# First attention: 1792 of 1857 softmax weights cross partitions by DMA, in runs of 448 keys

## The reference, cut to what matters

```python
k = (concat([ctx, x_normed]) @ Wk)      # 1857 keys, 4 groups of 128
v = (concat([ctx, x_normed]) @ Wv)
q = (x_normed @ Wq)                     # 32 heads of 128, 8 heads per group
scores = einsum('bqhgd,bkhd->bhgqk', q, k) / sqrt(128)
attn   = softmax(scores)                # float32
out    = einsum('bhgqk,bkhd->bqhgd', attn, v) @ Wo
```

## Time and profile before

| | |
|---|---|
| median of 3 runs | 3180.78 us (3176.02 to 3182.16) |
| the profiled execution | 3190.52 us, span 3188.8 us |
| its mean granted TensorE clock | 0.977 of full speed |
| busy shares of the span | PE 95%, PEld 85%, DVE 66%, ACT 54%, POOL 28% |
| DMA | 497 MB, 156 GB/s over the span |

### The profile page before, as it was taken

How to read it: one execution, slowest core, us unless ns; L and a number is a source line. 1 busy time by engine, 2 the same in 40 slices (tenths; PEclk the granted TensorE clock), 3 DMA queues, 4 the chain that set the end, 5 groups by cost and what they waited for, 6 DMA issues and landing times. The chain is left out here.

```text
span 3188.8 us, 54146 instructions
## 1 busy us (share of the span) xinstructions
PE 3040.3 (95%) x18566; PEld 2702.9 (85%) x18566; DVE 2104.0 (66%) x3215; ACT 1733.4 (54%) x3277; POOL 908.0 (28%) x742
## 2 busy tenths in 40 slices
PE   8999998999999999999999999979989799998897
PEld 7888887899999999899998999968768788886786
DVE  4433343788888888788887888854454567766675
ACT  4433344676666666666666666642243344443472
POOL 0000121344444444444444444432200124440101
PEclk9999999999999999999999999999989799999998
DMA  7665696766777776677766777557540111111683
GB/s 253 216 214 200 207 289 200 152 159 161 165 160 158 163 157 164 150 165 158 160 160 155 160 158 163 127 148 238 190 160 32 57 29 41 41 41 30 236 289 129
DMA packets 375894, 497.03 MB, mean 156 GB/s; under 512 B 34316, under 2 KB 283452, under 8 KB 375640
## 3 DMA queue, kind: packets, MB, share of 16 engines
q1 hardware_dynamic: 373080, 485.40, 56.8%
q0 software_dynamic: 2560, 8.39, 0.8%
HBM read 225.57 MB, written 133.87 MB: 113 GB/s over the span
## 5 line engine op out<-in xcount | busy, mean ns | idle before, releaser
L725 POOL TENSOR_TENSOR a_t_lo<-a_turned,a_t_hi 128x512 fp32r<-128x512 f32 x512 | 649.7, 1291 | 937.9 <-ACT a_t_hi L854 937.9
L845 ACT ACTIVATE a_probs<-a_ps_s,a_neg_max 128x1024 f32<-128x1024 f32 (+1 forms) x512 | 529.2, 1034 | 474.7 <-DVE a_neg_max L897 468.8
L890 DVE TENSOR_REDUCE a_half_max<-a_ps_s 128x1 f32<-128x1024 f32 (+1 forms) x512 | 571.1, 1115 | 190.9 <-PE a_ps_s L742 186.7
L740 PE MATMUL a_ps_s<-a_k_buf,a_q_buf 128*128 128x512 f32 (+1 forms) x1024 | 420.1, 410 | 17.9 <-ACT a_probs L845 11.9
L741 PE MATMUL a_ps_s<-a_k_buf,a_q_buf 128*128 128x512 f32 (+1 forms) x1024 | 385.7, 377 | 0.0
L742 PE MATMUL a_ps_s<-a_k_buf,a_q_buf 128*128 128x512 f32 (+1 forms) x1024 | 384.8, 376 | 0.0
L926 DVE TENSOR_TENSOR a_x_lo<-a_ps_x,a_x_hi 128x512 fp32r<-128x512 f32 (+1 forms) x512 | 314.3, 614 | 106.6 <-ACT a_x_hi L863 106.6
L916 DVE STREAM_TRANSPOSE a_turned<-xn 128x512 f32<-128x512 f32 x512 | 357.4, 698 | 0.0
L472 DVE TENSOR_TENSOR p_out<-p_ps_j,p_out 128x512 fp32r<-128x512 f32 (+3 forms) x196 | 153.3, 782 | 302.4 <-ACT p_out L400 302.4
L400 ACT ACTIVATE p_out<-p_ps_j 128x512 fp32r<-128x512 f32 (+3 forms) x196 | 141.9, 724 | 311.4 <-PE p_ps_j L293 311.4
L740 PE MATMUL a_ps_o<-a_t_hi,a_v_buf 128*128 128x256 f32 x1024 | 298.8, 292 | 6.1 <-issue 3.6
(11 more groups left out here) (394 smaller groups left out, 7102.0 us busy)
## 6 DMA issues: line engine op xcount, KB each, us to landing
xn<-a_probs SPq DMA_DIRECT2D x1024, 128.0 KB, 3.4
a_q_all<-p_out SPq DMA_DIRECT2D x64, 512.0 KB
a_q_buf<-a_q_all SPq DMA_DIRECT2D x128, 256.0 KB, 3.2
a_k_buf<-a_k_all SPq DMA_DIRECT2D x64, 464.5 KB, 4.0
a_v_all<-p_out SPq DMA_DIRECT2D x56, 512.0 KB
a_k_all<-p_out SPq DMA_DIRECT2D x48, 384.0 KB
a_v_buf<-a_v_all SPq DMA_DIRECT2D x64, 256.0 KB
a_o_all<-a_o_part SPq DMA_DIRECT2D x128, 128.0 KB, 3.1
```

Source lines behind the costliest of these rows:

```text
L725: pool.tensor_tensor(t_lo[:, slot, :, :], turned[:, slot, :, :], t_hi[:, slot, :, :].bitcast(F32), ALU.subtract).then_inc(t_done, 1)
L740: pe.matmul(o, w_hi, m_hi, start=first, stop=False)
L845: act.activation(probs[j][u.a][:, lo:hi], s_flat[:, lo:hi], ACT.Exp, bias=neg_max[:, j:j + 1], scale=SCALE, accum_out=half_sum[:, bass.ds( ...
L890: dve.reduce_max(half_max[:, half:half + 1], s_flat[:, lo:hi], AX.X).then_inc(max_done, 1)
```

## The change

The run grows from 256 to 448 keys, so 1792 keys go by the first way (seven steps per unit) and the last 65 by the second (one step, two transposes). The four DMAs per tile stay four, with rows of 1792 instead of 1024 bytes. `traded` gets a buffer of its own for odd units. The value loads become four of 32 partitions (14 blocks each) and one of 65. The rings of t_hi and t_lo keep four slots, that of x_hi and x_lo goes from four to two. A tile's transfers now wait for both halves of its exponentials. The output copy moves from VectorE to ScalarE, and every engine's order is rewritten. The core of the diff:

```diff
-    RUN = 256
+    RUN = 448
-    RING, PRING, XBANKS = 4, 4, 2
+    RING, PRING, XBANKS = 4, 2, 2
-    VALUE_PIECES = [(0, 1), (2, 3), (4,), (5, 6)]
+    VALUE_PIECES = [(0, 1), (2,), (3,), (4,)]
 load_values(sp, b, g, a, c):
-                elif c < RUNS + 2:
-                    lo, hi = [(0, VPLAIN), (VPLAIN, PLAIN - 1)][c - RUNS]
...
 trade(u, j):
-                    sp.wait_ge(probs_done, 4 * u.n + 2 * j + 1)
+                    sp.wait_ge(probs_done, 4 * u.n + 2 * j + 2)
 POOL step(b, r):
-                    w, l = Unit(b, r - 2), Unit(b, r - 3)
-                    low(l, 1)
-                    low(l, 2)
-                    low(l, 3)
-                    low(w, 0)
+                    for p in range(TPAIRS):
+                        low(Unit(b, r), p)
 TensorE step(b, r): v = r-1, w = r-2, l = r-3, z = r-4
+                    turn_plain(l, 0)
                     weigh_turned(z, 2)
-                    weigh_plain(z, 2)
-                    turn_plain(l, 1)
-                    weigh_plain(z, 3)
+                    weigh_turned(z, 3)
+                    weigh_turned(z, 4)
+                    weigh_turned(z, 5)
                     scores(v, 0, 0)
-                    turn_plain(l, 2)
                     scores(v, 0, 1)
-                    weigh_turned(z, 3, last=True)
-                    turn_plain(l, 3)
+                    weigh_turned(z, 6, last=True)
                     weigh_turned(l, 0, first=True)
                     weigh_plain(l, 0)
                     weigh_turned(l, 1)
                     scores(v, 1, 0)
-                    turn_plain(w, 0)
                     scores(v, 1, 1)
-                    weigh_plain(l, 1)
 ScalarE step(b, r): u = r, v = r-1, w = r-2, z = r-3
                     exponentials(v, 1, 0)
-                    plain_high(w, 1)
+                    plain_high(w, 0)
                     exponentials(v, 1, 1)
                     turned_high(w, 0)
                     turned_high(w, 1)
-                    plain_high(w, 2)
+                    turned_high(w, 2)
                     exponentials(u, 0, 0)
-                    plain_high(w, 3)
                     exponentials(u, 0, 1)
-                    turned_high(w, 2)
+                    take_output(z)
                     turned_high(w, 3)
-                    plain_high(v, 0)
+                    turned_high(w, 4)
+                    turned_high(w, 5)
+                    turned_high(w, 6)
 VectorE step(b, r): v = r-1, l = r-3
-                    plain_low(l, 1)
+                    turn_traded(l, 0)
                     turn_traded(l, 1)
+                    plain_low(l, 0)
+                    turn_traded(l, 2)
                     maximum(v, 0, 0)
                     maximum(v, 0, 1)
                     negate_maximum(v, 0)
-                    turn_traded(l, 2)
-                    take_output(z)
-                    plain_low(l, 2)
                     turn_traded(l, 3)
+                    turn_traded(l, 4)
+                    turn_traded(l, 5)
+                    turn_traded(l, 6)
                     maximum(v, 1, 0)
-                    plain_low(l, 3)
                     maximum(v, 1, 1)
                     negate_maximum(v, 1)
-                    plain_low(w, 0)
-                    turn_traded(w, 0)
```

More of the change, by code:

```diff
@@ L538, in grouped_attention_block @@
     pair_tiles = lambda e: range(2 * e, min(2 * e + 2, PLAIN))
-    RING, PRING, XBANKS = 4, 4, 2
+    RING, PRING, XBANKS = 4, 2, 2
     KPIECES = 4
-    VPLAIN = (PLAIN - 1) // 2
-    VALUE_PIECES = [(0, 1), (2, 3), (4,), (5, 6)]
+    VALUE_PIECES = [(0, 1), (2,), (3,), (4,)]
     PIECE = 2 * WIDTH // KPIECES
     VPIECES = sum(len(p) for p in VALUE_PIECES)
-    assert QT == 2 and len(CHUNKS) == 4 and HPG == 8 and TURNED <= 2 * BANK and TBLOCKS % 2 == 0 and WIDTH % 2 == 0
+    assert QT == 2 and len(CHUNKS) == 4 and HPG == 8 and TPAIRS == 7 and PPAIRS == 1 and TBLOCKS % 2 == 0 and WIDTH % 2 == 0
     assert PLAIN % 2 == 1 and TPAIRS * HEADS % RING == 0 and PPAIRS * HEADS % XBANKS == 0 and PPAIRS * HEADS % PRING == 0
@@ L582, in load_values @@
                                  keys_of[RUN * c:RUN * (c + 1), g, :].rearrange("(k i) d -> i k d", i=SQ)).then_inc(v_loaded[a], 16)
-                elif c < RUNS + 2:
-                    lo, hi = [(0, VPLAIN), (VPLAIN, PLAIN - 1)][c - RUNS]
-                    sp.dma_start(v_buf[a][:, TBLOCKS + lo:TBLOCKS + hi, :].bitcast(F32),
-                                 keys_of[TURNED + P * lo:TURNED + P * hi, g, :].rearrange("(m i) d -> i m d", i=P)
-                                 ).then_inc(v_loaded[a], 16)
                 else:
@@ L606, in grouped_attention_block @@
             probs = [[sb(f"probs{j}{a}", [P, KEYS]) for a in range(2)] for j in range(QT)]
-            traded = xn[:, :, :].rearrange("p t d -> p (t d)")[:, 0:2 * QT * TURNED].rearrange("p (a j g r) -> p a j g r", a=2, j=QT, g=RUNS)
+            by_run = lambda rows: rows.rearrange("p (j g r) -> p j g r", j=QT, g=RUNS)
+            traded = [by_run(xn[:, :, :].rearrange("p t d -> p (t d)")[:, 0:QT * TURNED]),
+                      by_run(sb("traded", [P, QT * TURNED])[:, :])]
             turned = sb("turned", [P, RING, 2, TOK])
@@ L663, in trade @@
                     for c in range(RUNS):
-                        sp.dma_start(traded[SQ * c:SQ * (c + 1), u.a, j, :, :], probs[j][u.a][:, RUN * c:RUN * (c + 1)]
+                        sp.dma_start(traded[u.a][SQ * c:SQ * (c + 1), j, :, :], probs[j][u.a][:, RUN * c:RUN * (c + 1)]
                                      ).then_inc(trade_done[j][u.a], 16)
@@ L728, in step @@
                 def step(b, r):
-                    w, l = Unit(b, r - 2), Unit(b, r - 3)
-                    low(l, 1)
-                    low(l, 2)
-                    low(l, 3)
-                    low(w, 0)
-                run(pool, step, 4)
+                    for p in range(TPAIRS):
+                        low(Unit(b, r), p)
+                run(pool, step, 0)
             @block.tensor
@@ L812, in step @@
                 def step(b, r):
-                    v, w, l, z = Unit(b, r - 1), Unit(b, r - 2), Unit(b, r - 3), Unit(b, r - 4)
+                    v, l, z = Unit(b, r - 1), Unit(b, r - 3), Unit(b, r - 4)
+                    turn_plain(l, 0)
                     weigh_turned(z, 2)
-                    weigh_plain(z, 2)
-                    turn_plain(l, 1)
-                    weigh_plain(z, 3)
+                    weigh_turned(z, 3)
+                    weigh_turned(z, 4)
+                    weigh_turned(z, 5)
                     scores(v, 0, 0)
-                    turn_plain(l, 2)
                     scores(v, 0, 1)
-                    weigh_turned(z, 3, last=True)
-                    turn_plain(l, 3)
+                    weigh_turned(z, 6, last=True)
                     weigh_turned(l, 0, first=True)
@@ L864, in plain_high, with take_output @@
                                    ).then_inc(x_hi_done, 1)
+                def take_output(u):
+                    if not u.live:
+                        return
+                    act.wait_ge(tv_ps, TPAIRS * (u.n + 1))
+                    act.wait_ge(xv_ps, PPAIRS * (u.n + 1))
+                    wait(act, o_stored[u.a], 16 * u.use)
+                    act.activation(o_part[:, u.a, :], ps_o[:, u.a, 0:TOK], ACT.Copy).then_inc(copy_done, 1)
                 def step(b, r):
-                    u, v, w = Unit(b, r), Unit(b, r - 1), Unit(b, r - 2)
+                    u, v, w, z = Unit(b, r), Unit(b, r - 1), Unit(b, r - 2), Unit(b, r - 3)
                     exponentials(v, 1, 0)
-                    plain_high(w, 1)
+                    plain_high(w, 0)
                     exponentials(v, 1, 1)
@@ L916, in turn_traded @@
                     dve.transpose(turned[:, slot, :, :].rearrange("p k (q r) -> p k q r", r=SQ),
-                                  traded[:, u.a, :, :, 2 * SQ * p:2 * SQ * (p + 1)].rearrange("p j g (k r) -> p k (j g) r", k=2)
+                                  traded[u.a][:, :, :, 2 * SQ * p:2 * SQ * (p + 1)].rearrange("p j g (k r) -> p k (j g) r", k=2)
                                   ).then_inc(turn_done, 1)
@@ L927, in plain_low @@
                                       x_hi[0:rows, slot, 0:m, :].bitcast(F32), ALU.subtract).then_inc(x_done, 1)
[L929 to L935, removed]
                 def step(b, r):
-                    v, w, l, z = Unit(b, r - 1), Unit(b, r - 2), Unit(b, r - 3), Unit(b, r - 4)
-                    plain_low(l, 1)
+                    v, l = Unit(b, r - 1), Unit(b, r - 3)
+                    turn_traded(l, 0)
                     turn_traded(l, 1)
+                    plain_low(l, 0)
+                    turn_traded(l, 2)
                     maximum(v, 0, 0)
```

## The result

The changed kernel takes 3382.07 us, the median of four executions (3370.67 to 3399.26), beside 3180.43 before; the ratio estimated from the runs is 1.0641, interval 1.059 to 1.0692. The 3382.07 us are 201.6 more than before, over 127 steps from unit to unit 1.59 us each, so a unit takes 12.12 + 1.59 = 13.71 us; in the traced execution it is 257.6 / 127 = 2.03 more than before, 14.15.

The account below looks back on a forecast made before the run. The prediction took the DMA to bound the changed kernel: weights 11.6, values 1.25 and 0.03, queries 0.78, output 0.39, keys 0.70, 14.75 us per unit; 2.63 more over 127 steps is +334, so 3515 us, range 3185 to 3600.

Parts of the forecast that it names:

- The step that decided: Softmax weights by DMA: time proportional to bytes, 0.83 x 1.75 = 1.45 us per transfer, 11.6 per unit; chance 0.58.
- The rival by the packet: Weights transfers: 1792-byte rows take little longer than 1024, so a unit takes 12.16 us, 3190 in all; chance 0.15.
- that of keys and values: DMA demand per unit: values 1.25 and 0.03 us, keys 0.70, added to the other transfers without overlap.
- the first three terms: DMA demand per unit: weights 11.6 us, queries 0.78 and output 0.39, added without overlap.
- the moved waits: SP issues a tile's transfers 0.93 us later, after its second exponentials; claimed hidden, or free when the queue is full.
- The new chain: Attention, scores to scores through exponentials, output copy, t_hi, POOL's t_lo and weighing: 12.16 us, taking back TensorE's gain.
- the faster case: Attention: cheap packets and t_lo 5 ready early leave 11.46 us per unit, -84 us, 3097; chance 0.10.
- the score loop: Attention: scores, maximum, exponentials, next scores, twice per unit; without transpose blocks 2 x (6.08 - 0.35) = 11.46 us.
- The case at the rate of the value loads: Rival: weights transfers with long rows run at 183 GB/s, a unit takes 13.15 us, +131, 3312; chance 0.17.
- What would show it: Signs: DMA share near 0.9 or above, TensorE idle, VectorE waiting at first transpose, landings 1.4 to 1.5 us apart, unit near 14.7.

Follow-up runs that it names:

- the order 0, 2, 1, 3: The changed kernel, whole, with a tile's four weights transfers issued in the order 0, 2, 1, 3: 3359.72 us, ratio 1.0551.
- 384 columns: The changed kernel with each weights transfer moving 384 of its 448 columns from the third unit on, product partly wrong: 3267.83 us, ratio 1.0297.
- 256 columns: The changed kernel with each weights transfer moving 256 of its 448 columns from the third unit on, part of product left out: 3170.58 us, ratio 0.9968.
- the copy moved: The changed kernel moving 256 of 448 columns, with ScalarE's output copy also moved from ahead of t_hi 3 to behind t_hi 6: 3142.67 us, ratio 0.9879.
- runs of 320: Whole kernel between both: 1280 keys by DMA, 577 by TensorE, three transfers per tile issued earlier, queries before second tile's weights: 3155.88 us, 0.9919 of the kernel before.
- the queries ahead: The changed kernel, whole, with a later unit's queries issued before the second tile's weights instead of behind them and the output: 3338.48 us, ratio 1.0508.

## Why the prediction was right, and what it mis-sized

**The step that decided was right.** The weights by DMA cost by the byte, and the DMA takes the place of TensorE as the bound. Without the added bytes the loss is gone (3170.58), and with all the bytes written to 128 partitions it is gone too (3165.07). So where a transfer writes decides, as I took it from the value loads beside the queries and the output; that it is the number of partitions, and not the four rows in each, isn't separated. The rival by the packet, at 3190, falls: the packets are the same in number in all these runs. The Trainium skill's rule ("SBUF — State Buffer", section "Door 1: The DMA port swizzle"), that 32 neighbouring partitions reach half of SBUF's DMA ports, agrees with the landings of 2.2 to 2.4 us beside 3.9 to 7.0. By the same section partitions 0 to 63 share one set of eight ports and 64 to 127 the other. One might take from this that transfers 0 and 2 of a tile run beside each other where 0 and 1 don't; the landings of the order 0, 2, 1, 3, 4.0 to 7.0 us beside 3.9 to 7.0, show nothing of it.

**The size was off: 14.75 us predicted, 13.71 measured, 3515 beside 3382.** The term of the sum that was too large, as far as the runs tell, is that of keys and values. The weights with the queries and the output were put at 11.6 + 0.78 + 0.39 = 12.77, and the kernel that loads no keys or values has 12.71. Keys and values were put at 1.25 + 0.03 + 0.70 = 1.98, and leaving them out saves 1.00. What failed is the sentence "I find no overlap between them in that sum, so I add them": it was read from a kernel whose queue rested a quarter of the time, where overlap changes nothing that one could see. That the first three terms come out so close is partly luck, two errors against each other: alone, a weights transfer took 1.67 us and not 1.45, and eight of 1.67 with the other terms would be 16.5 us, so 2.8 us of the unit of 13.71 must be overlap. With 384 columns the same sum gives 9.96 + 0.78 + 0.39 + 1.98 = 13.11, and the run has 12.12 + 86.7 / 127 = 12.80: 0.3 too much, where the overcharge of keys and values above is 1.0. So the sum isn't a law; near the engines' pace, units that are early can't pay for those that are late. Which transfers overlap, and by how much, is open.

**"When the queue is full anyway, this costs nothing more" was wrong.** It was said of the moved waits, with the queries named among what is queued behind them. I followed the weights to VectorE, and not the queries to TensorE: they landed 11.5 us behind their issue, and the scores waited 95 us in 1000 for them. Their place in the queue was worth 44 us. Here a full queue made the order in it a cost.

**The new chain and the faster case.** The chain was summed at 12.16 us. With 256 columns the unit is 12.12 - 10.1 / 127 = 12.04, TensorE waits for t_lo once in each unit, and taking the output copy out of the chain shortens it: the chain was there, and 0.1 too long. So what TensorE gave up was indeed taken back, by POOL's chain, before any transfer came into play. The faster case, 11.46 by the score loop alone, wasn't reached even with the copy moved: 12.12 - 38.4 / 127 = 11.82.

**The rivals.** The case at the rate of the value loads, 3312, lies nearer to the measured 3382 than my own 3515, by 70 us against 133; its reason, a faster transfer from longer rows, is wrong: alone, the longer rows went at 137 GB/s, under the 158 before.

**What would show it.** As listed: a DMA share above 0.9 with no empty slice (1.07), VectorE waiting at a unit's first transpose (109 us in 1000), TensorE idle. Not as listed: landings 1.67 us apart where the transfers run alone, not 1.4 to 1.5, and 13.71 us per unit, not 14.7; and TensorE's largest wait on a DMA was for the queries.

## What to carry to other kernels

Before work is moved from an engine to the DMA, price the transfer by the bytes and by the partitions that it writes, at the rate of the nearest transfer of the same kind, and look at which engine's gain is left once the next chain is counted: here there was at most 10 us to win as ordered and 200 to lose. When a queue fills, follow every tile that is in it to its reader, not only the one that you changed: here the queries, which the change didn't touch, were late too. A partial move, sized so that the transfers still land in time, with two changes of order, gained 24 us (runs of 320).

## What the runs showed of the hardware that was not expected

A DMA share of about 1 is no verdict. With runs of 320 it was 1.02 at 182 GB/s, and no wait of TensorE ended with a transfer; in the changed kernel it was 1.07 at 193 GB/s (1000 to 1200 us) and the kernel lost 202 us; with the queries ahead it was 1.07 at 201 GB/s. What tells is who waits for a landing, and for how long.

Longer rows were slower per byte when a tile's four transfers ran alone: 137 GB/s with rows of 1792 bytes, 158 with rows of 1024. The slow rate isn't there from the start. In the changed kernel the GB/s from 553 to 561 us, in slices of 0.2 us, are:

```profile
GB/s 0 0 0 0 0 0 0 0 63 403 367 224 117 117 179 125 108 116 143 161 90 126 135 161 134 116 99 179 134 99 108 135 179 108 116 134 161 134 100 184
```

The first transfer begins at 403 GB/s, and from 556 to 560 us, with several under way, the mean is 129. Why it falls isn't shown.

TensorE's clock fell where it waited. Four windows of the changed kernel, 4 us each, columns as in the earlier trace rows:

```profile
1512.00:1516.00 4.00, 3.57 (x21) 2.96 (x20) 3.16 (x5) 3.34 (x8) 1.62 (x2) 1.00 1.08 160
1516.00:1520.00 4.00, 2.90 (x22) 2.43 (x20) 0.73 (x2) 2.92 (x6) 3.40 (x3) 1.00 1.09 212
1520.00:1524.00 4.00, 1.65 (x5) 1.33 (x6) 2.22 (x4) 1.86 (x3) 1.99 (x2) 0.84 1.09 164
1524.00:1528.00 4.00, 4.00 (x22) 3.54 (x21) 2.36 (x3) 0.00 (x0) 1.76 (x2) 0.73 1.12 197
```

It was granted 1.00 (2.4 GHz) until TensorE stood for 3.17 us up to 1522.35, and 0.84 and 0.73 in the two windows in and behind this wait, so part of them at 1.2 GHz. In the kernel with runs of 320, where TensorE hardly waits, it is 1.00 from 1000 to 2000 us. The prediction said that TensorE's idling costs nothing; what the slower clock adds to a late unit wasn't measured by itself.
